# Moved waits, turns and transfers between the spline stage, the first feed-forward block and attention of a four-layer kernel

## The reference

```python
x = x + jnp.tanh(g_xattn[0]) * _L0_xattn_ref(_layernorm(x), ctx_2048, ctx_2048, Wi, bi, Wf, bf, ln_scale)
x = x + jnp.tanh(g_ffn[0]) * _L0_ffn_ref(_layernorm(x), gate_cp, up_cp, down_cp)
x = x + jnp.tanh(g_xattn[1]) * _L1_xattn_ref(_layernorm(x), ctx_2048, ctx_2048)
x = x + jnp.tanh(g_ffn[1]) * _L1_ffn_ref(_layernorm(x), gate_w, up_w, down_w)
```

## Time and profile before

| | us |
|---|---|
| three timed runs: median (lowest to highest) | 1417.8 (1411.62 to 1421.6) |
| the profiled execution's own time | 1409.09 |
| its span, first to last instruction | 1407.1 |
| TensorE busy | 1228.1 (87%) |
| VectorE busy | 1158.8 (82%) |
| ScalarE busy | 570.8 (41%) |
| GpSimd busy | 368.2 (26%) |
| mean granted TensorE clock | 0.939 |

### The profile page before, as it was taken

How to read it: one execution, slowest core, us unless ns; L and a number is a source line. 1 busy time by engine, 2 the same in 40 slices (tenths; PEclk the granted TensorE clock), 3 DMA queues, 4 the chain that set the end, 5 groups by cost and what they waited for, 6 DMA issues and landing times. The chain is left out here.

```text
span 1407.1 us, 17960 instructions
## 1 busy us (share of the span) xinstructions
PE 1228.1 (87%) x6504; PEld 584.1 (42%) x6528; DVE 1158.8 (82%) x1515; ACT 570.8 (41%) x951; POOL 368.2 (26%) x291
## 2 busy tenths in 40 slices
PE   4679999457899898996797888989999999999998
PEld 3358787331343343442122222334444444444444
DVE  7667778896889889998657768888989898999986
ACT  3344665445644444453474645322222223222212
POOL 0022433255533332311467777300000000000000
PEclk9889999775899999997799999999999999999999
DMA  9511033144834363343402306562222223222221
GB/s 297 182 66 61 12 121 106 61 133 158 254 100 140 100 170 90 90 120 99 96 12 68 57 17 117 103 108 46 45 45 51 54 52 67 45 45 45 45 59 39
DMA packets 180707, 125.88 MB, mean 89 GB/s; under 512 B 137999, under 2 KB 148903, under 8 KB 180508
## 3 DMA queue, kind: packets, MB, share of 16 engines
q1 hardware_dynamic: 179356, 120.75, 32.5%
q0 software_dynamic: 1280, 4.20, 1.0%
HBM read 61.15 MB, written 27.66 MB: 63 GB/s over the span
## 5 line engine op out<-in xcount | busy, mean ns | idle before, releaser
L1861 PE MATMUL FD<-W1H,HH 128*128 128x512 f16 x512 | 155.8, 386 | 8.0 <-DVE ROOM L1919 4.9
L2740 PE MATMUL HD<-W1H,HT 128*128 128x512 f16 x480 | 146.4, 382 | 2.9 <-DMA HT<-OS 2.9
L1775 POOL TENSOR_TENSOR HL<-ROOM,HH 128x512 f16<-128x512 f32 x48 | 74.2, 1545 | 157.9 <-ACT HH L1800 157.9
L2503 DVE TENSOR_REDUCE NQ<-A_M 128x2 f32<-128x1024 f32 x60 | 73.3, 1222 | 46.6 <-PE A_M L2372 46.3
L1855 PE MATMUL FG<-W1L,W1H 97*128 97x512 f16 x324 | 84.1, 384 | 22.6 <-DVE ROOM L1919 11.9
L2662 ACT CAST OS<-SS 128x2048 f16<-128x2048 f32 x14 | 26.6, 1899 | 182.1 <-DVEq L2834 182.1
L336 ACT ACTIVATE DD<-E,TM 128x128 f32<-128x128 f32 x256 | 72.7, 369 | 66.7 <-PE E L432 65.0
L1861 PE MATMUL FD<-W1H,HL 128*128 128x512 f16 x256 | 98.6, 385 | 0.0
L2324 ACT ACTIVATE PT<-A_S,CM 128x1024 f32<-128x1024 f32 x64 | 71.2, 1113 | 57.8 <-PE A_S L2398 57.8
L2740 PE MATMUL HD<-W1L,HT 128*128 128x512 f16 x240 | 91.7, 382 | 0.0
L2247 POOL TENSOR_TENSOR SS<-SS,PT 128x512 f32<-128x512 f32 x62 | 84.6, 1385 | 17.0 <-ACT PT L2324 12.6
(11 more groups left out here) (419 smaller groups left out, 2698.1 us busy)
## 6 DMA issues: line engine op xcount, KB each, us to landing
VALP<-in_ffn_weights_dram SPq DMA_DIRECT2D x24, 512.0 KB, 4.3
VALQ<-in_ffn_weights_dram SPq DMA_DIRECT2D x24, 512.0 KB
quantised_weights<-QQ SPq DMA_DIRECT2D x24, 512.0 KB, 5.1
X<-in_x_dram SPq DMA_DIRECT2D x8, 1024.0 KB, 6.3
W1L<-features_kept SPq DMA_DIRECT2D x16, 288.0 KB
CTX<-in_ctx_dram SPq DMA_DIRECT2D x4, 1024.0 KB, 6.9
features_kept<-W1L SPq DMA_DIRECT2D x4, 1024.0 KB, 5.3
down_weights<-NAT SPq DMA_DIRECT2D x4, 1024.0 KB, 4.2
```

What stands on the lines that cost most here:

```text
L1775: pool.tensor_tensor(HL[:, KI - 1 - i, :], HM[:, i % 2, :], HH[:, i, :], ALU.subtract).then_inc(hl_ready, 1)
L1861: last = pe.matmul(DN[c][:, :], lhs[:, at, c * P:(c + 1) * P], W2[:, i, part, :], start=(i == 0 and n == 0), stop=(i == KI - 1 and n == 2))
L2503: v.tensor_reduce(NQ[:, i % NC, at:at + 2], first_bank(g, i)[:, :, :], AX.X, ALU.max, negate=True).then_inc(mx_taken, 1)
L2740: ins = pe.matmul(DN[:, :], HT[:, lp, i, :], W[:, 2, i * D:(i + 1) * D], start=(i == 0 and lp == 0 and W is WH), stop=(i == KI - 1 and lp ...
```

## The change

- Spline stage: `scales` moves from unit 20 to unit 14; `inverses` 0 and 1 come in at units 16 and 17, and go from the first feed-forward.
- Opening of the first feed-forward: SP loads raw tile 0 only, then the features, then waits for the first 8 gathers and loads tiles 1 and 2. GpSimd issues the second 8 gathers only when all of `gate_up(0, ·)` is done. `down(0, c, 0)` waits for 14 products (c = 0, 1) or 15 (c = 2, 3), not for 16.
- Last stage: turns 2 and 3 go through the banks T, which held the features' transposes, and wait for no `values`; `entry.low` runs on VectorE at step 6, not on GpSimd.
- Attention: in even groups `negatives(g + 1)` comes ahead of the 128 x 1024 `low`.

```diff
+BLOCK_SCALE_UNIT = 14
+INVERSE_UNITS = (16, 17)
...
-                if u == SCALE_UNIT:
+                if u == BLOCK_SCALE_UNIT:
                     quantiser.scales(v)
+                if u in INVERSE_UNITS:
+                    quantiser.inverses(v, INVERSE_UNITS.index(u))
...
     def turn(self, pe, j, bank):
         pe.wait_ge(self.ctx_in, 16)
-        if j >= 2:
-            pe.wait_ge(self.vt_ready, j - 1)
...
-ENTRY = {"deviation": 0, "inverse": 1, "queries": 2, "high": 4, "low": 4, "turn": (7, 9), "values": (8, 10),
+ENTRY = {"deviation": 0, "inverse": 1, "queries": 2, "high": 4, "low": 6, "turn": (7, 9), "values": (8, 10),
...
             sp.wait_ge(nat_stored, 16 * (KI // 4))
-            for n in range(Q_SLOTS):
-                quantiser.load(sp, n)
+            quantiser.load(sp, 0)
             features.near_elements(sp, 1)
             features.near_moments(sp, 1)
+            sp.wait_ge(w2_loaded[0], 16 * KI // 2)
+            for n in range(1, Q_SLOTS):
+                quantiser.load(sp, n)
...
             for i in range(KI):
+                if i == KI // 2:
+                    pool.wait_ge(u_ready, KI)
                 pool.indirect_dma_start(W2[:, i, :, :].rearrange("p a c -> p (a c)"), None, natural,
...
-                    elif i == ENTRY["low"]:
-                        entry.low(pool)
...
-                                entry.values(act, 2 * ENTRY["values"].index(i) + j, GU[j])
+                                entry.values(act, 2 * ENTRY["values"].index(i) + j, (GU, T)[ENTRY["values"].index(i)][j])
...
-            pe.wait_ge(hm_ready, KI)
...
                         for c in range(NC):
+                            if i == 0 and s == 0:
+                                pe.wait_ge(hm_ready, KI - 2 + c // 2)
...
                         if i in ENTRY["turn"]:
+                            pe.wait_ge(hm_ready, B * KI)
+                            features.t_free(pe)
                             for j in range(2):
-                                pe.wait_ge(hm_ready, B * KI)
-                                entry.turn(pe, 2 * ENTRY["turn"].index(i) + j, GU[j])
+                                entry.turn(pe, 2 * ENTRY["turn"].index(i) + j, (GU, T)[ENTRY["turn"].index(i)][j])
...
-                if i in INVERSES:
-                    quantiser.inverses(v, INVERSES.index(i))
...
+                        if i == ENTRY["low"]:
+                            entry.low(v)
...
-                        if i == 7:
-                            low(b, slice(2, NC))
...
                 if g + 1 < QUADS:
                     negatives(g + 1)
+                if even:
+                    low(b, slice(2, NC))
```

More of the change, by code:

```diff
@@ L1335 @@
 LEAST = 1.5 * 2.0 ** 14
-INVERSES = (0, 8)
 def rounding_order():
@@ L1369, in __init__, with inverse_room, place @@
         self.scale_own = nc.alloc_semaphore("q_scale_own")
-    def place(self, nc, A, CO, store, stack):
+    def inverse_room(self, nc, CO):
+        self.inverse_ready = nc.alloc_semaphore("q_inverse")
+        self.IV = CO[:, :, :, :].rearrange("p t n f -> p (t n f)")[:, 0:2 * QTILES * QT // BLK].rearrange(
+            "p (n k) -> p n k", k=QT // BLK)
+    def place(self, nc, A, store, stack):
         def sb(name, shape, dt=F32):
@@ L1376, in place @@
         self.MAG, self.LEAST = sb("MAGQ", [P, QT]), sb("LEASTQ", [P, 1])
-        self.IV = CO[:, :, :, :].rearrange("p t n f -> p (t n f)")[:, 0:2 * QTILES * QT // BLK].rearrange(
-            "p (n k) -> p n k", k=QT // BLK)
         self.VAL = sb("VALQ", [P, Q_SLOTS, QT])
@@ L1383, in place @@
         self.stored = [sem(f"q_stored{i}") for i in range(2)]
-        (self.inverse_ready, self.least_ready, self.exponent_ready, self.bound_ready, self.rounded_ready, self.val_ready, self.qh_ready,
+        (self.least_ready, self.exponent_ready, self.bound_ready, self.rounded_ready, self.val_ready, self.qh_ready,
          self.ql_ready, self.own) = (sem("q_" + n) for n in (
-             "inverse", "least", "exponent", "bound", "rounded", "val", "qh", "ql", "own"))
+             "least", "exponent", "bound", "rounded", "val", "qh", "ql", "own"))
     def load(self, sp, n):
@@ L1674, in high, with low @@
         self.nc.scalar.copy(self.Q2[:, 0, 0, :, :], self.XN[:, :, :]).then_inc(self.qh_ready, 1)
-    def low(self, pool):
-        pool.wait_ge(self.qh_ready, 1)
-        pool.tensor_tensor(self.Q2[:, 0, 1, :, :], self.XN[:, :, :], self.Q2[:, 0, 0, :, :], ALU.subtract).then_inc(self.ql_ready, 1)
+    def low(self, v):
+        v.wait_ge(self.qh_ready, 1)
+        v.tensor_tensor(self.Q2[:, 0, 1, :, :], self.XN[:, :, :], self.Q2[:, 0, 0, :, :], ALU.subtract).then_inc(self.ql_ready, 1)
     def scales(self, v):
@@ L3069, in build_program @@
             features = Features(nc, A, X, MV, RS, CST[:, 0:P], features_kept, WL, weights)
+            quantiser.inverse_room(nc, CO)
             with ExitStack() as stack:
@@ L3073, in build_program @@
             with ExitStack() as stack:
-                quantiser.place(nc, A, CO, store, stack)
+                quantiser.place(nc, A, store, stack)
                 ffn0_phase(nc, A, X, TG, IDH[:, :], GW, W2, natural, nat_stored, IDX, idx_loaded, features, SCL,
```

## The result

| | us |
|---|---|
| before, seven timed runs: median (lowest to highest) | 1417.8 (1411.6 to 1421.6) |
| changed, seven timed runs: median (lowest to highest) | 1403.5 (1399.9 to 1405.5) |
| ratio, 95% interval | 0.990 (0.987 to 0.992) |
| profiled execution of the changed kernel | 1405.5 (before: 1409.1) |

The median fell by 14.3 us (11 to 18 by the interval); 9.4 had been forecast. The profiled executions differ by only 3.6. So the first thing to read is where each execution spends its time. *Opening* runs from the spline stage's barrier to batch 1's first product, *middle* from there to the first addition of stage 2, *last* from there to the next barrier.

A forecast was written before the change was run, and what follows sets the result against it. VectorE and TensorE were each taken as close to full in stage 0, VectorE setting the last stage. +1.2 - 3.0 - 1.5 - 6.1 = -9.4 us took the median from 1417.8 to 1408.4, range 1401 to 1414.

The forecast's parts named there:

- rival 2: All goes well: the opening's stop goes and all four parts reach their good bounds; -14.0 us, time 1403.8; chance 13%.
- B: Opening of the first feed-forward: inverses gone from between products, shorter TensorE wait, transfers hidden; -3.0 us.
- D: Attention: negatives ahead of the keys' low half save the smaller of wait and operation in groups 0, 2, 4; -6.1 us.
- the 8.7 us: Profiled execution before lies this far under the timed median; claimed untouched by the change, so the median goes 1417.8 to 1408.4.
- The single stop of 1.40 us: Opening: VectorE and ScalarE stop together at 379.80, unexplained by the trace; priced at nothing, 1.4 us as upper bound.
- A: Spline stage: scales hidden at unit 14, inverses at units 16 and 17 delay later copies; +1.2 us, bounds 0.8 and 2.0.
- C: Last stage: VectorE sets it, then SP's last store holds the barrier; -1.5 us.
- Rival 3: Last stage: TensorE's 10.3 us wait is worth its full length; time 1399.6 us; chance 5%.
- The bounds of -0.7 and -2.3: Last stage: bounds stated for how far the barrier moves, around the forecast -1.5 us.
- the row's bounds of 1.2 and 4.25 us: Last stage: bounds on the moved `entry.low` operation's time on VectorE, taken as 2.4 us.
- The spread of 1407.6 to 1409.2: Whole kernel: the forecast median's own spread in us, from the bounds of A and C.
- Rival 1: Attention: casts meet GpSimd's sums and run slow; D only -3.1, sum -6.4, time 1411.4 us; chance 13%.

The follow-up runs named there:

- first eight experiments: Five kernels with part of the edits, two with single lines of the transfers' edit or one taken back, and the changed kernel repeated; kernel before there 1422.6 or 1420.6 us.
- last stage alone: Kernel before with only the last stage's edit: turns 2 and 3 in banks T, `entry.low` on VectorE; median 1419.6 us against 1422.6, ratio 0.998.
- gathers split alone: Kernel before with one line: GpSimd's second 8 gathers wait for the last gate-and-up product; median 1414.1 us against 1420.6, ratio 0.995.
- Before again: The unchanged kernel before, profiled a second time on another chip; median 1411.4 us, ratio 0.999.
- transfers alone: Kernel before with second 8 gathers and raw tiles 1 and 2 delayed, and the finer `down(0, c, 0)` wait; median 1412.6 us against 1422.6, ratio 0.991.
- inverses alone: Kernel before with scales moved and inverses placed in the spline stage, none in the opening, transfers as before; median 1423.6 us against 1422.6, ratio 1.000.

## Why the prediction was right and where it was wrong

The time came inside the range, 4.9 us below the forecast. The median fell by 1.01%, on the edge between "within 1%" (78%) and "faster by over 1%" (17%), and the interval of 0.987 to 0.992 doesn't decide. The time came out at the sum of rival 2, for a reason that this rival held only in part. That the sum came so near is partly luck: B fell short by 2.6 us, and the shorter stops and D gave more than that back in the median.

**The step that failed** is the sentence that nothing in the change touches the 8.7 us between the profiled execution and the median. It was one of before's fastest, in two places. 4.6 us are the first stage, 282.1 us against 286.7 on average in the other 13 profiles, mostly at a lower clock. The change indeed doesn't touch it: the changed profile has 287.1. The others are the stops. The seven profiles with a row of 16 gathers, two of them of the kernel before itself, have openings of 36.1, 38.7, 47.8, 43.0, 38.6, 42.8 and 35.3 us, 40.3 on average. The four with 8 and 8 have 34.2 to 37.0, 35.8 on average. The single stop of 1.40 us stood for a much larger term: on the two chips of the first eight experiments the five rows of 16 average 42.2 us, 6.4 more than the rows of 8. The prediction saw it, saw the transfer engines 93% busy, and priced it at nothing with 1.4 as its upper bound. A bound taken from one execution of a thing that the trace doesn't explain is no bound. The range of the timed runs before, 10 us in three runs, all of them above the profiled one, was the sign of it.

**A, forecast +1.2, measured +1.9 (1.7 on average).** The scales are hidden, as said. The size missed by the scaling behind the first pair: 1.05 us in the rows above, where the earlier trace rows leaves 0.4 between the reciprocal and the next product. It runs beside a subtraction on GpSimd, and the one behind the second pair, at 348.76, runs beside none and takes 0.35. GpSimd's timeline of the changed kernel:

```profile
344.56 1.15 POOL L1088 TENSOR_TENSOR NAT<-ROOM,NAT 128x512 f16<-128x512 f32 x1 [1.62 <-ACT NAT L1094]
347.35 1.16 POOL L1088 TENSOR_TENSOR NAT<-ROOM,NAT 128x512 f16<-128x512 f32 x1 [1.63 <-ACT NAT L1094]
```

The rule on the shared pair of ports that the prediction took from the Trainium skill ("SBUF — State Buffer", section "Who interferes with whom") fits this.

**B, forecast -3.0, measured -0.4 in the two first profiles.** Its terms were right: the first product 0.35 us sooner, the step with the inverse 2.0 us shorter, the step across the bound 0.5 us shorter. Against them stood 1.7 us between the first and the third product, for which VectorE waited for TensorE (1.11 and 0.75 us), and a stop 0.8 us longer. TensorE ran at a granted clock of 0.64 over the first 9.6 us, where the profile of before had 0.81 over 9.5. Part of this is chance: the second profile of the changed kernel has 0.76 over its first 9 us and no such wait at the third product, and its opening is 34.2 us against 35.3 in the second profile of before, so B is -1.1 there. The features and the tiles were never waited for.

**C, forecast -1.5, measured -1.8.** TensorE had no wait between turns, VectorE's new operation took 2.29 (2.4 forecast), and the barrier is SP's. Rival 3 is refuted by the last stage alone. The bounds of -0.7 and -2.3 don't follow from the row's bounds of 1.2 and 4.25 us: 663.2 - 3.0 + 4.25 = 664.4 and 663.2 - 3.0 + 1.2 = 661.4 are +0.3 and -2.7 against 664.1. The spread of 1407.6 to 1409.2 takes one part's bound at a time; A and C together, as stated, give 1407.2 to 1410.0.

**D, forecast -6.1, measured -7.9 by the means (6.5 to 8.1 by single pairs).** The mechanism was right, the size too small. The waits kept 3.2 us and not 2.0; the first of the two casts still takes 1.2 us at the ends of groups 0, 2 and 4, as it did before. But attention became shorter by more than the waits did, and the granted clock of those stretches was 1.00 instead of 0.91 to 0.96. So a wait of TensorE seems to cost more than its length here, through the clock behind it; that term was missing. Rival 1 came in one of the three groups: the second cast takes 1.20 us at the end of group 0 and 0.18 at the ends of 2 and 4. In the kernel before it was group 2 that had the slow one (1.19 us), so on balance nothing was lost by it. VectorE's timeline of the changed kernel:

```profile
704.15 1.18 DVE L2517 CAST HB<-NQ 128x16 bf16<-128x16 f32 x1
705.36 1.20 DVE L2520 CAST NP<-HB 128x16 f32<-128x16 bf16 x1
...
754.80 1.22 DVE L2517 CAST HB<-NQ 128x16 bf16<-128x16 f32 x1
756.05 0.18 DVE L2520 CAST NP<-HB 128x16 f32<-128x16 bf16 x1
```

**Rival 4** exists, but did not decide: 1.3 us at the third product when the second gathers end 42 us behind the barrier, nothing when they end at 36.5 or, in the gathers split alone, at 38.3. The prediction let the cost begin at 396 - 352.5 = 43.5 us, 2 to 5 us too late.

The sum by the measured terms is 1.9 - 1.8 - 7.9 = -7.8 for A, C and D, and -4.5 or more for the opening, inverses and stops together. That is -12.3, inside the 11 to 18 measured. The 4.5 is a difference of means over several chips, with openings of 35.3 to 47.8 us on one side, so the sum is no closer than a few us.

## What to carry to other kernels

If the profiled execution is faster than every timed run, ask first which part of it was lucky. A second profile need not show it: that of the unchanged kernel, on another chip, had no stop either, and only profiles of other kernels with the same opening did. Gathers of GpSimd are not free merely because nobody waits for their data: try them spaced, and with the loads out of their stretch. When a wait of TensorE is taken away, look at the granted clock behind it as well as at its length.

## What the runs showed of the hardware that was not expected

- While GpSimd issues indirect transfers back to back, 1.25 us apart, and the transfer engines are about full, VectorE, ScalarE and TensorE can all stop for 1 to 8 us at a time, with nothing in the trace that they wait for. On VectorE the stops begin 7 us behind the first gather or later, and the last of them ends 1.8 to 4.2 us behind the issue of a row's last gather. In all four profiles with rows of 8 there is one, of 1.5 to 2.2 us, at the eighth. The one profile with a row of 16 on the chip of "Before again" showed none, and none of the three with spaced gathers did. Whether the engines' semaphores or their instruction supply is stopped, no run tells. Against the second speaks that in the last stage alone the only packet of the instruction queues in the opening lies 32 to 36 us behind the barrier, after the last stop. The Trainium skill ("SBUF — State Buffer", section "Who interferes with whom") says that TensorE and ScalarE never wait on anyone for the ports and that no transfer contends with a compute engine; if so, it is not the ports. No run here tests that.
- The time varies from one execution to the next on the same chip. With the row of 16 the changed kernel spreads over 15.6 us (12 runs), with 8 and 8 over 3.8 and 5.7 (6 and 7), and spaced over 5.4, 5.0 and 3.1 (6 each). It is not a rule that the row sets the spread: the transfers alone, with 8 and 8, spread over 13.7 (6), and the inverses alone, with 16, over 7.0 (12).
- The first stage, the same code in all 14 profiles, took 282.1 to 287.9 us. In eleven of them the granted clock falls to between 0.59 and 0.83 for ten us between 100 and 120 us; the two shortest, 282.1 and 283.6, and before again (285.8) have 1.00 there.
